# Graph layer kernel: the residual's own part leaves the first stage for the edge stage, and the set-up work of the first stage moves behind its last statistics

## The reference, cut to what matters

```python
h = jnp.maximum(_layernorm(x, axis=-1), 0.0)            # 6250 x 256
# _L0_gnn_ref, called with x = h; self loops carry a zero edge_attr
e = jax.nn.relu(ea @ ee_w1 + ee_b1) @ ee_w2 + ee_b2
msg = x[src] + e
agg = jax.ops.segment_sum(msg, dst, num_segments=n)
h = (1.0 + eps) * x + agg                               # then a three-layer MLP per node
```

## Time and profile before

| | us |
|---|---|
| median of three runs (lowest, highest) | 3161.82 (3158.79, 3163.97) |
| span of the profiled execution | 3157.3 |
| first stage, to the edge stage's first instruction | 93.03 |
| POOL's first gather of the edge stage, start | 94.14 |
| POOL's last gather, end | 1098.37 |

### The profile page before, as it was taken

The page is one execution under the profiler, slowest core; times in us unless marked ns, Lnnn a source line. Parts: engine busy times, 40 slices in busy tenths (PEclk is TensorE's granted clock), DMA queues, the critical chain, the costliest instruction groups (busy, mean ns, idle before and its releaser), DMA issues. The chain is left out here.

```text
span 3157.3 us, 79016 instructions
## 1 busy us (share of the span) xinstructions
PE 2446.9 (77%) x25310; PEld 2164.9 (69%) x25311; DVE 2156.6 (68%) x3833; ACT 1488.6 (47%) x3803; POOL 1976.9 (63%) x2143
## 2 busy tenths in 40 slices
PE   0577777777777789999999999947777777777763
PEld 0466666666666679999999999945555555555552
DVE  7676667777677636666666666657766766666666
ACT  5444444444444458888888888831111111111114
POOL 4677777777777634444444444437777777777772
PEclk9998889999899889999999999978888888887996
DMA  6555555555555500000000000026555655555554
GB/s 158 168 161 149 158 154 166 161 163 160 159 164 158 143 25 18 21 21 20 20 21 20 20 22 21 21 61 178 171 173 173 174 172 168 173 172 173 171 170 136
DMA packets 183839, 373.69 MB, mean 118 GB/s; under 512 B 42598, under 2 KB 93688, under 8 KB 183769
## 3 DMA queue, kind: packets, MB, share of 16 engines
q0 software_dynamic: 75552, 209.66, 23.5%
q1 hardware_dynamic: 107392, 162.37, 17.4%
q10 hardware_dynamic: 824, 0.87, 0.1%
HBM read 346.95 MB, written 25.80 MB: 118 GB/s over the span
## 5 line engine op out<-in xcount | busy, mean ns | idle before, releaser
L446 POOL DMA_INDIRECT rows<-tab_scratch,srcs x784 | 765.7, 977 | 238.7 <-issue 234.1
L1458 POOL DMA_INDIRECT a_rows<-tab_scratch,srcs x784 | 750.5, 957 | 251.7 <-issue 235.8
L1524 PE MATMUL sum_ps<-feat,a_hot 128*125 128x264 f32 x1960 | 601.5, 463 | 237.5 <-DVE feat L1616 121.0
L1524 PEld LDWEIGHTS sum_ps<-feat,a_hot 128*125 128x125 f32 x1960 | 417.4, 222 | 341.7 <-DVE feat L1616 133.9
L876 PE MATMUL z_ps<-ah,w 128*128 128x125 f16 x6400 | 553.8, 219 | 1.0 <-PEq L982 1.0
L876 PE MATMUL z_ps<-al,w 128*128 128x125 f16 x3200 | 542.7, 217 | 0.0
L876 PEld LDWEIGHTS z_ps<-ah,w 128*128 128x128 f16 x6400 | 489.5, 97 | 1.5 <-issue 1.4
L1468 ACT ACTIVATE feat<-d 128x32 f32<-128x32 f32 x196 | 44.9, 229 | 827.0 <-DVE d L1612 566.2
L500 PE MATMUL mlp_ps<-ewa,eab 128*128 128x256 f16 x788 | 203.5, 290 | 284.3 <-PEq L496 283.3
L478 ACT ACTIVATE rh<-mlp_ps 128x1024 f16<-128x1024 f32 x196 | 199.7, 1019 | 358.2 <-ACTq L477 347.7
L829 POOL TENSOR_TENSOR a<-a 128x500 f32<-128x500 f32 x100 | 124.4, 1244 | 372.1 <-POOLq L828 372.1
(11 more groups left out here) (211 smaller groups left out, 5422.8 us busy)
## 6 DMA issues: line engine op xcount, KB each, us to landing
ea<-edge_t SPq DMA_DIRECT2D x394, 128.0 KB
dstb<-dst_flat SPq DMA_DIRECT2D x98, 512.0 KB
rows<-tab_scratch,srcs POOLq DMA_INDIRECT x784
a_rows<-tab_scratch,srcs POOLq DMA_INDIRECT x784
tab_scratch<-prow SPq DMA_DIRECT2D x50, 128.9 KB
hx<-x SPq DMA_DIRECT2D x50, 125.0 KB
x_scratch<-x SPq DMA_DIRECT2D x50, 125.0 KB
hs<-tab_scratch SPq DMA_DIRECT2D x50, 125.0 KB
```

The costliest lines, as they stand in the source:

```text
L446: pool.indirect_dma_start(rows[:, b % DEEP, k, :], None, dram["tab0"], bass.IndirectOffsetOnAxis(ap=srcs[:, c:c + 1], axis=0),).then_inc(r ...
L1458: pool.indirect_dma_start(rows[:, b % DEEP, k, :], None, dram["tab1"], bass.IndirectOffsetOnAxis(ap=srcs[:, c:c + 1], axis=0),).then_inc(r ...
L1524: ins = pe.matmul(out[:], hot[:, h, k, :], feat[:, row, k, :], start=(k == 0), stop=(k == CB - 1))
```

## The change

`own` leaves `prepare`. In its place `edges0` gets ten instructions (`own_terms`), one a chunk, that compute `(2 + eps) * acc + ee_b2` on `acc`, on DVE behind the one-hot of batch 1; their last raises `chain_sem`, so that the first addition of edge sums comes behind them. `ee_b2` lies in a corner of the still empty weight buffer `w` during `prepare`, and a copy of it in PSUM serves `own_terms`. DVE's round becomes `stats(c+1)`, `low(c-2)`, `coefficients(c+1)`. The set-up work stands in the last round that has statistics behind it (`c == CH - 1`), ahead of `low(7)`, with fewer `settled` waits. SP issues the first eight table stores ahead of the schedule's six small ones.

```diff
             sp.dma_start(sb["srcs"][:], t["src_cols"]).then_inc(stored, 16)
+            def table(c):
+                sp.wait_ge(tb_ready, c + 1)
+                for rows in splits:
+                    sp.dma_start(tb_v[rows, tiles(c), :], tb[rows, c % 2]).then_inc(tb_stored[c % 2], 16)
+            for c in range(CH - 2):
+                table(c)
             sp.wait_ge(sched_ready, 1)
...
-            for c in range(CH):
-                sp.wait_ge(tb_ready, c + 1)
-                for rows in splits:
-                    sp.dma_start(tb_v[rows, tiles(c), :], tb[rows, c % 2]).then_inc(tb_stored[c % 2], 16)
+            for c in range(CH - 2, CH):
+                table(c)
...
-            def own(c):
-                h = acc[0:TN, tiles(c), 0:D]
-                dve.wait_ge(t_ready, c + 1)
-                settled(dve.scalar_tensor_tensor(out=h, in0=h, scalar=eps1[0:TN, :], in1=ht[:, c % 2], op0=ALU.mult, op1=ALU.add))
...
             stats(0)
             coefficients(0)
-            settled(dve.tensor_tensor(cmp_[:], ...))
...
             for c in range(CH + 2):
+                if c + 1 < CH:
+                    stats(c + 1)
+                if c == CH - 1:
+                    edge_weights()
+                    schedule()
                 if c >= 2:
                     low(c - 2)
-                if 1 <= c < CH:
-                    own(c - 1)
                 if c + 1 < CH:
-                    stats(c + 1)
                     coefficients(c + 1)
-            own(CH - 1)
...
             dve.tensor_copy(iota_ps, iota16[:])
+            dve.tensor_copy(b2_ps, sb["b2bc"])
...
             main_hot(0, 0, tiles_of(nc, DVE, table, 0, 1)[0][0])
-            dve.sem_inc(chain_sem, 1)
             low_parts(0)
+            def own_terms():
+                for c in range(NT // PG):
+                    h = acc[0:TN, c * PG:(c + 1) * PG, 0:D]
+                    ins = dve.scalar_tensor_tensor(out=h, in0=h, scalar=sb["eps2"][0:TN, :],
+                                                   in1=b2_ps.unsqueeze(1).broadcast_to([TN, PG, D]), op0=ALU.mult, op1=ALU.add)
+                ins.then_inc(chain_sem, 1)
...
                         main_hot(b + 1, 1 - s, tiles[u + 2][0])
+                        own_terms()
```

More of the change, by code:

```diff
@@ L84, in build @@
             with ExitStack() as edge_mlp:
-                for name, shape, dt in [("ewa", [P, D], F16), ("ewb", [ED + 2, D], F16), ("dsts", [P, NCH + CB], F32)]:
+                for name, shape, dt in [("ewa", [P, D], F16), ("ewb", [ED + 2, D], F16), ("dsts", [P, NCH + CB], F32),
+                                        ("eps2", [P, 1], F32)]:
                     sb[name] = Memory(nc, edge_mlp).sb(name, shape, dt)
+                sb["b2bc"] = sb["w"][0:TN, WROWS - 1, 0, 0:2 * D].bitcast(F32)
                 stale = prepare(nc, t, dram, sb)
@@ L126, in prepare @@
         thr = m.sb("thr", [P, NT - 1], F32)
-        b2bc = m.sb("p_b2bc", [TN, D], F32)
-        eps1 = m.sb("eps1", [P, 1], F32)
+        b2bc, eps2 = sb["b2bc"], sb["eps2"]
         er = m.sb("er", [P, D], F32)
@@ L200, in _ @@
                     pool.wait_ge(t_free, c - 1)
-                pool.tensor_tensor(ht[:, c % 2], acc[0:TN, tiles(c), 0:D], b2bc[:].unsqueeze(1).broadcast_to([TN, PG, D]),
+                pool.tensor_tensor(ht[:, c % 2], acc[0:TN, tiles(c), 0:D], b2bc.unsqueeze(1).broadcast_to([TN, PG, D]),
                                    ALU.add).then_inc(t_ready, 1)
@@ L206, in _ @@
         def _(act):
-            act.dma_start(b2bc[:], t["L0_gnn_ee_b2"].partition_broadcast(TN)).then_inc(ld_small, 16)
+            act.dma_start(b2bc, t["L0_gnn_ee_b2"].partition_broadcast(TN)).then_inc(ld_small, 16)
             act.dma_start(er[0:ED, :], t["L0_gnn_ee_w1"]).then_inc(ld_small, 16)
@@ L211, in _ @@
             act.dma_start(ebr[ED:ED + 2, :], t["L0_gnn_ee_b1"].partition_broadcast(2)).then_inc(ld_small, 16)
-            act.dma_start(eps1[:], t["L0_gnn_eps"].partition_broadcast(P)).then_inc(ld_small, 16)
+            act.dma_start(eps2[:], t["L0_gnn_eps"].partition_broadcast(P)).then_inc(ld_small, 16)
             def deviation(c):
@@ L286, in low @@
                 dve.sem_inc(t_free, 1)
[L288 to L295, removed]
@@ L296, in _, with schedule @@
-            settled(dve.tensor_tensor(sb["ewb"][:], ebr[:], ebh[:], ALU.subtract))
-            dve.sem_inc(eb_split, 1)
+            def schedule():
+                dve.wait_ge(ld_dst, 16)
+                for j in range(2):
+                    dve.tensor_reduce(ext[:, j:j + 1], drow[:, j, :], AX, ALU.min)
+                    ins = dve.tensor_reduce(ext[:, 2 + j:3 + j], drow[:, j, :], AX, ALU.max)
+                settled(ins)
+                settled(dve.tensor_tensor(cmp_[:], ext[:].unsqueeze(2).broadcast_to([half, 4, NT - 1]),
+                                          thr[0:half, :].unsqueeze(1).broadcast_to([half, 4, NT - 1]), ALU.is_ge))
+                settled(dve.tensor_reduce(tile[:], cmp_[:], AX, ALU.add))
+                dve.tensor_copy(sched_sb[:, 0, :], tile[:, 0:2])
+                settled(dve.tensor_scalar(sched_sb[:, 1, :], tile[:, 2:4], 1.0, None, ALU.add))
+                dve.tensor_copy(spans_sb[:], sched_sb[:].rearrange("p c j -> p j c")).then_inc(sched_ready, 1)
@@ L298, in _, with edge_weights @@
+            def edge_weights():
+                dve.wait_ge(ld_small, 16 * 6)
+                dve.tensor_scalar(eps2[:], eps2[:], 2.0, None, ALU.add)
+                dve.tensor_copy(sb["ewa"][:], er[:])
+                settled(dve.tensor_copy(ebh[:], ebr[:]))
+                settled(dve.tensor_tensor(sb["ewb"][:], ebr[:], ebh[:], ALU.subtract))
+                dve.sem_inc(eb_split, 1)
             stats(0)
             coefficients(0)
-            settled(dve.tensor_tensor(cmp_[:], ext[:].unsqueeze(2).broadcast_to([half, 4, NT - 1]),
-                                      thr[0:half, :].unsqueeze(1).broadcast_to([half, 4, NT - 1]), ALU.is_ge))
@@ L302, in _ @@
[L302 to L305, removed]
-            for c in range(CH + 2):
+            for c in range(CH + 2):
+                if c + 1 < CH:
[3 more added lines that the diff above has]
+                    schedule()
@@ L370, in edges0 @@
         sum_ps = m.ps("sum_ps", [TN, 3, 2 * D])
-        iota_ps = m.ps("e_iota_ps", [P, TN])[:]
+        const_ps = m.ps("e_const_ps", [P, TN + D])
+        iota_ps, b2_ps = const_ps[:, 0:TN], const_ps[0:TN, TN:TN + D]
         ld_tab = m.sem("ld_tab")
```

## The result

The changed kernel is slower: median 3167.72 us of 9 runs against 3159.43 us of 9 runs of the kernel before; ratio 1.0024, 95% interval 1.0014 to 1.0033, that is 7.6 us (4.4 to 10.4); the two medians alone lie 8.3 us apart. The profiled execution has a span of 3163.5 us against 3157.3. Of these 6.2 us the first stage makes 5.29; the edge stage's gathers take 0.6 less, the stages behind it 1.6 more, which no part of the change touches (their length differs by up to 5.7 us among the profiles of all kernels told of here).

The account below looks back on a forecast made before the run. DVE's order was taken to bound the first stage's rounds, POOL's 784 gathers the edge stage. Gate -0.7, rounds +1.95, tail +5.4 and edge stage +1.0 gave +7.65 us, 3169.5 us; own range 3166 to 3174, 8 in 10 3160 to 3175.

Parts of the forecast that it names:

- Five rounds: First stage, coefficients 4 to 9: nmr waits for POOL's whole addition, rounds of 7.03 us instead of 6.64, +1.95 us.
- second rival: First-stage rounds: nmr slips in ahead of POOL, rounds near 5.0 us, sum -0.5 us, 3161.3 us; chance 0.16.
- Tail: First stage from the last nmr to its end: the set-up now stands ahead of low(7), +5.4 us.
- my two orders: Tail: POOL's last addition starts first, 18.9 us, or low(8) does, 19.8; against 13.93, 4.9 to 5.9 more.
- nothing: Tail: price given to SP's six small transfers between the stores of chunks 7 and 8, about 2 us of issuing.
- Store gate: First stage's beginning, high half of chunk 2 waiting for chunk 0's store: 0.7 us earlier, bounds 2.1 earlier, 0.5 later.
- Edge stage: Start of the edge stage: ten own terms, about 15.5 us on DVE, cost +1.0 us, bounds nothing and 4 us.
- the cover: Edge stage: POOL's lead of 14.0 us at its 25th gather, against a delay of 13.9 us by the own terms.
- Sum: Whole kernel: gate, rounds, tail and edge stage together, +7.65 us, median 3169.5 us.
- the third: Rival in the edge stage: the lead doesn't cover the own terms, 6 us on top, 3175.5 us; chance 0.07.
- The fourth: Faster rival: nmr not held up, gate opens 2.1 us earlier, tail's set-up hidden, -8.8 us, 3153 us; chance 0.07.

Follow-up runs that it names:

- the slot given back behind nmr: Changed kernel with `t_free` raised after the coefficients, so POOL gets the slot of `ht` behind nmr; ratio 1.0013 against the kernel before.
- set-up early: Changed kernel with schedule and edge weights back ahead of the first statistics; ratio 1.0015 against the kernel before.
- only SP's order: Kernel before, with only the first eight table stores put ahead of the schedule's six small transfers; ratio 0.9992.
- own terms spread: Changed kernel with slot given back behind nmr, set-up early and the ten own terms spread over the edge stage; 3150.1 us, ratio 0.9971 against the kernel before.
- the move alone: Kernel before, with only the own part moved out of the first stage and spread over the edge stage; ratio 0.9981.
- both edits: Changed kernel with the slot given back to POOL behind nmr and the set-up ahead of the first statistics; ratio 0.9986 against the kernel before.

## Why the prediction was right, point by point

- *Five rounds*, forecast +1.95 us, measured +1.29. The mechanism is as worked out: nmr waits for the whole addition. The round is 6.89, not 7.03, since the low half need not wait for the result of the last statistics instruction (51.36 + 0.45 against 51.72 in the same round, 0.1 us). The experiment with the slot given back behind nmr shows the cause; the second rival's round of 5.0 is nearly what that edit gives.
- *Tail*, forecast +5.4, measured +7.24. Set-up 5.9 for 6.2, and low(8) did go first, which was the dearer of my two orders (5.9). What I missed is a wait that takes over: with low(7) late, the store of chunk 7 is late, and the last high half waits for it 2.0 us longer than for POOL. I had dismissed the six small transfers as "nothing". In four versions that issue them right behind the store of chunk 7 (the changed kernel, set-up early, only SP's order, own terms spread) it lands 6.1 to 6.6 us behind the end of low(7); with the move alone, which issues them early, it has landed at most 4.2 us behind, and POOL releases the last high half.
- *Store gate*, forecast -0.7, measured -3.24, outside my bounds of -2.1 to +0.5. The step that failed is the pricing of the six small transfers by SP's issuing time. SP's order alone moved the gate by 2.6 us, though the store was issued only 1.4 us earlier (31.57 for 32.98). And of two stores that are issued at the same moment, the one with the small transfers ahead of it lands 3.25 us later. First the timeline of the move alone, where they stand ahead, then that of both edits with the own terms spread, where they come later:

```profile
33.29 50.43 SPq L176 DMA_DIRECT2D tab_scratch<-tb  x20
...
43.89 1.27 ACT L234 ACTIVATE tb<-ht 125x1280 f16<-125x1280 f32 x1 [6.19 <-DMA tab_scratch<-tb]
```

```profile
33.30 37.73 SPq L176 DMA_DIRECT2D tab_scratch<-tb  x16
...
40.64 1.27 ACT L236 ACTIVATE tb<-ht 125x1280 f16<-125x1280 f32 x1 [4.04 <-DMA tab_scratch<-tb]
```

So the landing does depend on the queue more than on the issue, as the prediction says; what it left out is that the small transfers are part of that queue.

- *Edge stage*, forecast +1.0, bounds 0 and 4. In the profiled execution the cover held at the 25th gather and fell short by 1.4 us at the 37th, the batch with an extra tile. Over many runs the block cost more: of kernels with nearly one first stage (83.4 to 83.9 us) two with the block gained 4.4 and 5.1 us, the spread one 9.2, the one without 7.3. The other runs say the same. Take from a kernel's difference to the kernel before the part that its first stage explains: 2.3 us are left for the changed kernel and 4 to 5 for the four others with this block, against -0.3 to 0.6 for the four with spread terms and 2.4 for the one without them. Each figure is good to some 3 us. So the term was nearer 4 than 1, at the upper end of its bounds. Where the rest beyond the waits of 0.6 to 1.9 us goes stays open: the profiles of one execution each differ by some us in the lengths of the gathers alone (762.6 to 769.1 us busy).
- *Sum*: +7.65 forecast, 7.6 by the ratio. (The forecast of 3169.5 us stood on a median of three runs, 3161.82; over nine it is 3159.43, so only the difference can be compared.) In the first stage the gate came out 2.5 us and the rounds 0.7 below the forecast, the tail 1.8 above: 5.3 for 6.65. The ratio leaves 2.3 us for the rest, where the edge stage was to cost 1.0. So the mechanisms of rounds and tail were right, but that the total met its number is luck: its errors cancelled.

The second rival did not come about, nor did the third at its price, though the spread version shows a part of it. The fourth's condition, a hidden tail and an open gate, is what the version with both edits and spread own terms makes by other means: 3150.1 us, faster than both kernels.

## What to carry to other kernels

Where two engines exclude each other, look at which of them a semaphore lets go first: here a tiny instruction that reached its start 0.3 us behind a long one of the other engine waited for nearly that one's whole length, and giving the semaphore a few instructions later gained it back. Work moved out of an idle place into the last round of a pipeline was paid nearly in full, and what came late next was a store two steps on. A block of work as long as the lead that hides it was not quite free, about 4 us of 14.7, and of 12 us more 9.8 were paid; spread along the stage the same work cost nothing that these runs can tell.

## What the runs showed that I had not expected

Six transfers of under 2 KB each, the larger ones in 100 rows of 8 or 16 bytes, made the table store beside them land 2.6 us later (41.33 against 43.93), or about 4 us later when ACT's queue sent them right behind its issue (45.05 against 40.5 to 41.9 in the versions that issue them behind the eighth store; in that run SP's last load was also issued 1.1 us later than in the version it was made from, 31.55 against 30.49). That is more than their 2 us of issuing. The small packets themselves are short: with the move alone, 301 packets of 8 or 16 bytes start between 35.2 and 39.0 us and take 9 ns each. But the 1 KB packets that start from 38 to 44 us take 99 ns on average, against 54 ns at the same time with the own terms spread, where the small ones come later. Why such pieces slow the packets behind them was not tried further.
